# Perceiver block on one core: first attention's scores from four 64-row matmuls instead of three 128-row ones

## The chip, the cores and the metric

One core of a Trainium2 chip runs the whole block as one program. The time is the device time of the slowest core in microseconds, here of the only core. TensorE is PE in the rows (PEld its weight loads), VectorE DVE, ScalarE ACT, GpSimd POOL, SyncE SP.

## The reference, cut to what matters

The input x is 16 batches of 64 rows by 512, the context 16 batches of 512 rows by 512. A cross attention with 16 heads of 64, a self attention with 16 heads of 32, and a mixture of 8 experts (top 2) follow each other, each with a residual. The change touches the first attention's scores, and in the experts the place of one step:

```python
x = x + xattn(layernorm(x), ctx, ctx, ...)
    q = (query @ Wq + bq); k = (key @ Wk + bk); v = (value @ Wv + bv)
    scores = einsum('bqhd,bkhd->bhqk', q, k) / 8
    attn = softmax(scores); out = einsum('bhqk,bkhd->bqhd', attn, v)
x = x + attn(layernorm(x), ...)
x = x + ffn(layernorm(x), ...)
    h = gelu(x @ W1[e] + b1[e]); y = h @ W2[e] + b2[e]
```

## The kernel before, in words

Products are made at more than one pass's precision: each operand is split into a high part (fp32r) and a low part, and `split_pairs` (line 170) lists for each product high by high, high by low and low by high. `products` (line 405) issues them, so every logical 128x128x512 product is three matmuls.

**First attention** (lines 549 to 563). A pair of heads (128 columns of K) of one batch is one step; there are NS = 128 steps, 8 a batch. For step n TensorE runs, in this order: `project_k(n)` (12 matmuls of 512 columns into bank n % 2), `scores(n-1)` (3 matmuls), `project_v(n+4)` (12 matmuls, while n < 124), in every fourth step `weigh` (64 small matmuls of 64 columns, weights of 128 rows by 64 columns), and `turn(n-2)` (4 transposes of the probabilities into bank 6). For the scores the queries of a batch lie in `qbd`: for pair j a 128x128 matrix, the first head's queries in rows 0 to 63 and columns 0 to 63, the second head's in rows 64 to 127 and columns 64 to 127, zeros elsewhere, once as high and once as low part. Three matmuls of it with K (high, low) give the scores of both heads at once, 128x512, in bank 4 + n % 2. Two banks take turns.

ScalarE's order in step n (lines 1263 to 1297): at a batch's first step two splits of the next context (L1201), K's high part out of its bank (L1276), the exponential of scores n-1 (L1282, with the sum of each row), at a batch's third step `build_qbd` for the next batch (two copies of 64x512, L1252), in every fourth step the high part of `weigh`'s result (L1257), the copy of the transposed probabilities (L1292). VectorE's (lines 906 to 928): K's low part (L910), the row maximum of scores n-1 straight from the bank (L915), reciprocal and scaling (L917, L919), V out of its bank with its bias (L890), `build_qbd`'s low parts (L879), the low part of `weigh`'s result (L900). GpSimd splits the context and stores low parts. All order is by semaphores: `s_psum` (scores made), `s_max`, `s_exp`, `p_done` (probabilities ready), `k_lo`, `v_done`, `qbd_hi`, `qbd_lo`, `qbd_zero`.

**Experts.** A job is one expert: 16 tiles of the hidden width. In tile i TensorE runs `up` (12 matmuls as wide as the expert has rows, rounded up to one of eight widths), `down` of tile i - 3 (3 matmuls a 128 rows). Between them the next expert's rows are turned: `turned_at` (line 249) says after which tile each of the four 128-row chunks is transposed (`turn_rows`, line 715; ScalarE's copy `rows_high`, L1415; VectorE's `rows_low`, L1141). All four use bank 7, so chunk c waits for chunk c-1 to be out. The rows are gathered by GpSimd's queue (`fetch_rows`, L1588) into `xg`, which is also the tile that the expert before sends its results from (L1601), so the gather starts when those have been sent. ScalarE and VectorE also split the next expert's weights (L1201, L827), loaded tile by tile on SP's queue (L270).

Of the kernel before, what the change touches and what calls it, by code (L numbers as in the profile page):

```python
# [7 lines left out]
F32 = mybir.dt.float32  # L8
F32R = mybir.dt.float32r
# [3 lines left out]
ALU = mybir.AluOpType  # L13
ACT = mybir.ActivationFunctionType
AX = mybir.AxisListType.X
KB = 1024
P = 128


def perceiver_block(nc, a, out):  # L20

    B, TB, D = 16, 64, 512
# [4 lines left out]
    H1, HD1 = 16, 64  # L27
    HV = H1 * HD1
    NJ = HV // P
# [8 lines left out]
    with ExitStack() as stack:  # L38
        base = -(-nc.sbuf_base // 64) * 64

        def place(name, kb, shape, dt=F32):
            return nc.alloc_sbuf_tensor_at(name, shape, dt, offset=base + int(kb * KB))

        psum = stack.enter_context(nc.psum_tensor("psum", [P, 8, 512], F32))
        bank = [psum[:, i, :] for i in range(8)]
# [45 lines left out]
        o = c0 + 108  # L91
# [3 lines left out]
        xnT = [place(f"xnT{i}", o + 32 + 16 * i, [P, KD, T], F32R) for i in range(2)]  # L95
        Wq = [place(f"Wq{i}", o + 64 + 16 * i, [P, KD, HV], F32R) for i in range(2)]

        qbd = [[place(f"qbd{r}{i}", o + 32 + 8 * r + 4 * i, [P, NJ, P], F32R) for i in range(2)] for r in range(2)]
        kT = [[place(f"kT{r}{i}", o + 48 + 4 * r + 2 * i, [P, NKEY], F32R) for i in range(2)] for r in range(2)]
        V = [place(f"V{r}", o + 56 + 8 * r, [P, NKT, 512]) for r in range(3)]  # L100
        Pr = [place(f"Pr{r}", o + 80 + 2 * r, [P, NKEY]) for r in range(2)]
# [68 lines left out]
        def split_pairs(lhs, rhs):  # L170

            return [p for (lh, ll), (rh, rl) in zip(lhs, rhs) for p in ((lh, rh), (lh, rl), (ll, rh))]

        def pair(x, *idx):
            return (x[0][idx], x[1][idx])
# [71 lines left out]
        LAG = 3  # L247

        def turned_at(i):
            return {7: 0, 9: 1, 11: 2, 13: 3}.get(i)  # L250

        def d_on(i, k):
            return 0 <= i - k < NT
# [150 lines left out]
        def tensor_program(pe):  # L404
            def products(dst, pairs):
                for n, (l, r) in enumerate(pairs):
                    mm = pe.matmul(dst, l, r, start=n == 0, stop=n == len(pairs) - 1)  # L407
                return mm
# [89 lines left out]
            def scores(n):  # L498
                b, j = divmod(n, NJ)
                if j == 0:  # L500
                    pe.wait_ge(qbd_lo, 2 * b + 2)
                pe.wait_ge(k_lo, n + 1)
                if n >= 2:
                    pe.wait_ge(s_exp, n - 1)
                else:
                    pe.wait_ge(v_done, 3 + n)
                products(bank[4 + n % 2], split_pairs([pair(qbd[b % 2], slice(None), j)], [(kT[n % 2][0][:], kT[n % 2][1][:])])
                         ).then_inc(s_psum, 1)

            def turn(n):  # L510
                pe.wait_ge(p_done, n + 1)
# [19 lines left out]
            def c_product(t):  # L531
                rows = slice(t * P, (t + 1) * P)
                pe.wait_ge(low_in[t % 4], 16 * (t // 4 + 1))
                if t == 0:
                    loaded(*range(L_WO, L_WO + 4))
                if t < 2:
                    pe.wait_ge(v_done, NS)
                elif t < 4:
                    pe.wait_ge(k_lo, NS)
                elif t < 6:  # L540
                    pe.wait_ge(s_exp, NS)
                elif t == 6:
                    pe.wait_ge(pT_done, NS)
                else:
                    pe.wait_ge(o_lo, NS // HALF)
                products(c_bank(t), split_pairs([(Ohi[:, j, rows], oT[t % 4][:, j, :]) for j in range(NJ)],
                                                  [pair(Wo, slice(None), j) for j in range(NJ)])).then_inc(c_psum, 1)
# [273 lines left out]
        def vector_program(v):  # L821
# [47 lines left out]
                    split_lo(L_WK + j - 5, Wk[1][:, j - 5, :], Wk[0][:, j - 5, :])  # L869
            v.wait_ge(q_psum, 2 * NJ)  # L870
            for r in range(2):
                for i in range(2):
                    v.memset(qbd[r][i][:].bitcast(F32), 0.0).then_inc(qbd_zero, 1)

            def build_qbd(b):
                for h in range(2):
                    rows, cols = slice(64 * h, 64 * h + 64), slice(64 * h, 64 * h + 64)
                    v.wait_ge(qbd_hi, 2 * b + h + 1)
                    v.tensor_tensor(qbd[b % 2][1][rows, :, cols], QO[rows, :, b * TB:(b + 1) * TB], qbd[b % 2][0][rows, :, cols],  # L879
                                    ALU.subtract).then_inc(qbd_lo, 1)  # L880

            def evict_v(n):
                u, kt = divmod(n, HALF)
                cs = slice((u % 2) * 512, (u % 2) * 512 + 512)
                v.wait_ge(v_psum, n + 1)
                if n == 0:
                    v.wait_ge(bv_in, 16)
                if u >= 3 and kt == 0:
                    v.wait_ge(o_psum, HALF * (u - 2))
                v.tensor_tensor(V[u % 3][:, kt, :], bank[2 + (n if n < HALF else n % 2)], bvb[:, cs], ALU.add).then_inc(v_done, 1)  # L890
# [8 lines left out]
                    v.wait_ge(low_out[u % 4], 16 * (u // 4))  # L899
                v.tensor_tensor(Olo[u % 4][:], bank[7][:, 0:HALF * TB].rearrange("p (s q) -> p s q", s=HALF), hi, ALU.subtract).then_inc(o_lo, 1)  # L900

            v.wait_ge(qbd_zero, 4)
            build_qbd(0)
            for n in range(HALF):
                evict_v(n)
            for n in range(NS + 1):
                b, j = divmod(n, NJ)
                if n < NS:
                    v.wait_ge(k_hi, n + 1)
                    v.scalar_tensor_tensor(kT[n % 2][1][:], bank[n % 2], bkc[:, j:j + 1], kT[n % 2][0][:], ALU.add, ALU.subtract  # L910
                                           ).then_inc(k_lo, 1)
                if n >= 1:
                    m, r = n - 1, (n - 1) % 3
                    v.wait_ge(s_psum, m + 1)
                    v.tensor_reduce(smn[:, r:r + 1], bank[4 + m % 2], AX, ALU.max, negate=True).then_inc(s_max, 1)  # L915
                    v.wait_ge(s_exp, m + 1)
                    v.reciprocal(srec[:, r:r + 1], ssum[:, r:r + 1]).then_inc(s_recip, 1)  # L917
                    v.wait_ge(s_recip, m + 1)
                    v.tensor_scalar(Pr[m % 2][:], Pr[m % 2][:], srec[:, r:r + 1], None, ALU.mult).then_inc(p_done, 1)  # L919
                if n + HALF < NS:  # L920
                    evict_v(n + HALF)
                if j == 2 and b + 1 < B:
                    build_qbd(b + 1)
                if n >= 6 and n % HALF == 2:
                    o_low(n // HALF - 1)
                if n in (NS - 4, NS - 2):
                    for c in (n - NS + 4, n - NS + 5):
                        split_lo(L_WO + c, Wo[1][:, 2 * c:2 * c + 2, :], Wo[0][:, 2 * c:2 * c + 2, :])
# [267 lines left out]
        def scalar_program(s):  # L1196
# [50 lines left out]
            def build_qbd(b):  # L1247
                if b >= 2:
                    s.wait_ge(s_psum, NJ * (b - 1))
                for h in range(2):  # L1250
                    rows, cols = slice(64 * h, 64 * h + 64), slice(64 * h, 64 * h + 64)
                    s.activation(qbd[b % 2][0][rows, :, cols], QO[rows, :, b * TB:(b + 1) * TB], ACT.Copy).then_inc(qbd_hi, 1)  # L1252

            def o_high(u):
                b, half = divmod(u, 2)
# [2 lines left out]
                             ACT.Copy).then_inc(o_hi, 1)  # L1258

            s.wait_ge(q_done, 2 * NJ)  # L1260
            s.wait_ge(qbd_zero, 4)
            build_qbd(0)
            for n in range(NS + 3):
                b, j = divmod(n, NJ)
                if n < NS:
                    if j == 0 and b + 1 < B:
                        if n:
                            s.wait_ge(k_psum, n)
                            s.wait_ge(v_psum, n)
                        else:  # L1270
                            s.wait_ge(norm_out, 16)
                        ctx_high(b + 1)
                    s.wait_ge(k_psum, n + 1)
                    if n >= 2:
                        s.wait_ge(s_psum, n - 1)
                    s.activation(kT[n % 2][0][:], bank[n % 2], ACT.Identity, bias=bkc[:, j:j + 1]).then_inc(k_hi, 1)  # L1276
                if 0 <= n - 1 < NS:
                    m, r = n - 1, (n - 1) % 3
                    s.wait_ge(s_max, m + 1)
                    if m >= 2:  # L1280
                        s.wait_ge(pT_psum, m - 1)
                    s.activation(Pr[m % 2][:], bank[4 + m % 2], ACT.Exp, bias=smn[:, r:r + 1], accum_out=ssum[:, r:r + 1]).then_inc(s_exp, 1)  # L1282
                if n < NS and j == 2 and b + 1 < B:
                    build_qbd(b + 1)
                if n >= 6 and n % HALF == 2 and n < NS + 2:
                    o_high(n // HALF - 1)
                if 0 <= n - 2 < NS:
                    m = n - 2
                    s.wait_ge(pT_psum, m + 1)
                    if m >= HALF:  # L1290
                        s.wait_ge(o_psum, m - HALF + 1)
                    s.activation(PT[m % HALF][:], bank[6], ACT.Copy).then_inc(pT_done, 1)  # L1292
                if n in (NS - 4, NS - 2):
                    if n == NS - 4:
                        s.wait_ge(v_psum, NS)
                    for c in (n - NS + 4, n - NS + 5):
                        split_high(L_WO + c, Wo[0][:, 2 * c:2 * c + 2, :])
# [412 lines left out]
```

## Time and profile before

| | us |
|---|---|
| runs shown (3) | 1736.29, 1738.79, 1741.46; median 1738.79 |
| profiled execution, its own time | 1740.04 |
| its span in the trace | 1738.2 |
| PE / PEld / DVE / ACT / POOL busy | 1650.6 / 1391.5 / 881.5 / 696.1 / 307.2 |
| mean granted TensorE clock | 0.973 of full |

The profiled execution lies 1.25 us above the median of the runs, and its span 1.8 us below its own time. Busy time of PE counts a matmul from its start to its modelled end (389 ns for 512 columns), though the next may start 227 ns after it; what a matmul takes of the span is read from starts. Stages in the order of time: query projection to 49 us, first attention to 977, output product and second attention to 1210, experts to 1738.

### The profile page before, as it was taken

Reading aid. Unit: us, or ns where it says so; the run is one execution under the profiler, and the core shown is the slowest. Engines: PE = TensorE matmul, PEld = TensorE weight load, DVE = VectorE, ACT = ScalarE, POOL = GpSimd, SP = SyncE. Lnnn points to the kernel's source line nnn. Section 1 sums busy time; section 2 is a strip of 40 time slices with the busy share of each in tenths; the row PEclk is TensorE's granted clock in tenths of the full one; section 3 lists DMA queues with packets and bytes.
Section 4 is the critical chain, followed back from the end, with each engine's and each line's share of the span. In section 5 each row is a group of like instructions: output and inputs, shape, how many; then the busy total and the mean of one; then the engine's idle time right before and its main releaser. Section 6 shows DMA issues by size and latency. Waiting matters only on the chain. (4 is left out here: it accounts for less than half of the span.)

```text
span 1738.2 us, 26944 instructions
## 1 busy us (share of the span) xinstructions
PE 1650.6 (95%) x10858; PEld 1391.5 (80%) x10858; DVE 881.5 (51%) x1592; ACT 696.1 (40%) x1314; POOL 307.2 (18%) x258
## 2 busy tenths in 40 slices
PE   7999999999999999999999987995899999999987
PEld 6888888888888888888888766774888888888876
DVE  4344434443444434443443575785777457548842
ACT  5333333333333333333333433453655345436531
POOL 3201210011101110111010061465311011101101
PEclk9999999999999999999999998996899999999799
DMA  6601830111011101111002460113756336537621
GB/s 222 203 31 52 130 75 7 53 56 53 8 51 56 52 20 40 55 52 39 24 4 80 147 195 25 51 57 124 261 155 213 127 97 225 152 92 232 211 50 21
DMA packets 54101, 165.16 MB, mean 95 GB/s; under 512 B 10612, under 2 KB 10996, under 8 KB 53408
## 3 DMA queue, kind: packets, MB, share of 16 engines
q1 hardware_dynamic: 38032, 131.88, 22.3%
q0 software_dynamic: 15920, 31.19, 8.5%
q8 instruction: 106, 1.74, 0.4%
q14 instruction: 43, 0.35, 0.1%
HBM read 143.54 MB, written 55.64 MB: 115 GB/s over the span
## 5 line engine op out<-in xcount | busy, mean ns | idle before, releaser
L407 PE MATMUL psum<-ctx,Wk 128*128 128x512 f32 x1536 | 384.9, 399 | 0.0
L407 PE MATMUL psum<-Wv,ctx 128*128 128x512 f32 x1536 | 368.7, 389 | 0.0
L407 PEld LDWEIGHTS psum<-Wv,ctx 128*128 128x128 f32 x1536 | 288.3, 188 | 59.7
L407 PEld LDWEIGHTS psum<-ctx,Wk 128*128 128x128 f32 x1536 | 279.2, 188 | 55.5
L910 DVE SCALAR_TENSOR_TENSOR kT<-psum,bkc,kT 128x512 fp32r<-128x512 f32 x128 | 96.0, 750 | 387.7 <-ACT kT L1276 387.7
L407 PE MATMUL psum<-xgT,Wh 128*128 128x224 f32 (+5 forms) x1536 | 253.6, 319 | 13.1 <-issue 13.1
L407 PEld LDWEIGHTS psum<-xgT,Wh 128*128 128x128 f32 x1536 | 232.0, 200 | 30.9 <-issue 15.9
L748 PE MATMUL psum<-Wh,hs 128*128 128x512 f32 x981 | 246.4, 396 | 0.0
L748 PEld LDWEIGHTS psum<-Wh,hs 128*128 128x128 f32 x981 | 181.4, 191 | 34.1 <-DVE hs L1164 0.4
L1276 ACT ACTIVATE kT<-psum,bkc 128x512 fp32r<-128x512 f32 x128 | 88.3, 690 | 247.1 <-PE psum L407 247.0
L1441 ACT ACTIVATE gl<-psum,b1c 128x512 f32<-128x512 f32 x128 | 87.8, 686 | 211.5 <-PE psum L407 211.5
L1282 ACT ACTIVATE Pr<-psum,smn 128x512 f32<-128x512 f32 x128 | 88.2, 689 | 186.0 <-DVE smn L915 186.0
L827 DVE TENSOR_TENSOR Wh<-raw,Wh 128x1024 fp32r<-128x1024 f32 x128 | 155.6, 1219 | 7.1 <-ACT Wh L1201 6.9
L1504 POOL DMA_DIRECT2D low_parts<-Olo x32 | 24.5, 767 | 712.0 <-DVE Olo L900 712.0
L1201 ACT ACTIVATE Wh<-raw 128x1024 fp32r<-128x1024 f32 x128 | 134.4, 1054 | 26.8 <-DMA raw<-in_W 26.2
L1162 DVE CAST hs<-gl 128x512 fp32r<-128x512 f32 x128 | 55.3, 432 | 137.3 <-ACT gl L1441 136.6
L1292 ACT ACTIVATE PT<-psum 128x512 f32<-128x512 f32 x128 | 76.6, 598 | 97.0 <-PE psum L412 97.0
L407 PE MATMUL psum<-kT,qbd 128*128 128x512 f32 x384 | 107.9, 389 | 0.0
L1601 POOL DMA_INDIRECT out_x<-xg,meta x22 | 36.9, 1676 | 390.1 <-DVE xg L1154 387.4
L1477 POOL TENSOR_TENSOR ctx<-raw,ctx 128x1024 fp32r<-128x1024 f32 x32 | 76.1, 2399 | 113.1 <-ACT ctx L1201 113.1
L1164 DVE TENSOR_TENSOR hs<-gl,hs 128x512 fp32r<-128x512 f32 x128 | 88.7, 693 | 4.4
L890 DVE TENSOR_TENSOR V<-psum,bvb 128x512 f32<-128x512 f32 x128 | 87.4, 683 | 3.5 <-PE psum L407 3.5
(149 smaller groups left out, 1787.0 us busy)
## 6 DMA issues: line engine op xcount, KB each, us to landing
raw<-in_W SPq DMA_DIRECT2D x128, 512.0 KB, 3.8
expert_rows<-in_spare_rows SPq DMA_DIRECT2D x16, 1042.0 KB, 7.4
raw<-in_ctxT SPq DMA_DIRECT2D x32, 512.0 KB, 4.4
xg<-expert_rows POOLq DMA_DIRECT2D x32, 256.0 KB, 5.6
low_parts<-Olo POOLq DMA_DIRECT2D x32, 128.0 KB, 2.4
oT<-low_parts SPq DMA_DIRECT2D x8, 512.0 KB, 5.1
out_x<-x SPq DMA_DIRECT2D x12, 256.0 KB, 2.2
xs<-in_x SPq DMA_DIRECT2D x4, 512.0 KB, 6.8
```

The source lines that it names most:

```text
L407: mm = pe.matmul(dst, l, r, start=n == 0, stop=n == len(pairs) - 1)
L748: mm = pe.matmul(bank[3 + c], hr[x][:, c * P:(c + 1) * P], Wh[i][y][:, 512:1024], start=i == 0 and m == 0, stop=i == NI - 1 and m == 2)
L827: v.tensor_tensor(lo, src, hi, ALU.subtract).then_inc(split_done[r], 1)
L890: v.tensor_tensor(V[u % 3][:, kt, :], bank[2 + (n if n < HALF else n % 2)], bvb[:, cs], ALU.add).then_inc(v_done, 1)
L910: v.scalar_tensor_tensor(kT[n % 2][1][:], bank[n % 2], bkc[:, j:j + 1], kT[n % 2][0][:], ALU.add, ALU.subtract).then_inc(k_lo, 1)
L1164: v.tensor_tensor(lo, gl[n % HS][:], hi, ALU.subtract).then_inc(h_lo, 1)
L1201: s.activation(hi, src, ACT.Copy).then_inc(split_hi, 1)
L1276: s.activation(kT[n % 2][0][:], bank[n % 2], ACT.Identity, bias=bkc[:, j:j + 1]).then_inc(k_hi, 1)
L1282: s.activation(Pr[m % 2][:], bank[4 + m % 2], ACT.Exp, bias=smn[:, r:r + 1], accum_out=ssum[:, r:r + 1]).then_inc(s_exp, 1)
L1292: s.activation(PT[m % HALF][:], bank[6], ACT.Copy).then_inc(pT_done, 1)
L1441: s.activation(gl[n % HS][:], bank[n % 3], ACT.Gelu, bias=b1c[:, col:col + 1]).then_inc(gelu_done, 1)
L1477: g.tensor_tensor(lo, src, hi, ALU.subtract).then_inc(split_done[r], 1)
```

## The change

It rearranges the operands of the scores. `qbd` keeps only the high parts (block-diagonal, zeros elsewhere). A new `qx` holds in each 64-row half the same high part in the head's own columns and the low part in the other head's columns. For each head h the rows 64h to 64h+63 alone are multiplied: `qx` with K's high part, then `qbd` with K's low part, both into bank 4 + h. So a bank holds a head's scores in its own 64 partitions and the part low by high in the other 64. ScalarE copies that part across to the head's partitions of `Pr`, VectorE adds the two, and takes the maximum from `Pr`; the exponential reads `Pr` too. Banks 4 and 5 serve every step, no longer turn by turn. V's eviction stands ahead of reciprocal and scaling in VectorE's order. In the experts each chunk of rows is turned one tile later. `s_max` now counts three a step (two additions and the maximum), `s_exp` three (two copies and the exponential), `qbd_hi` four a batch.

```diff
-        qbd = [[place(f"qbd{r}{i}", ...) for i in range(2)] for r in range(2)]
+        qbd = [place(f"qbd{r}", o + 32 + 8 * r, [P, NJ, P], F32R) for r in range(2)]
+        qx = [place(f"qx{r}", o + 36 + 8 * r, [P, NJ, P], F32R) for r in range(2)]
...
         def turned_at(i):
-            return {7: 0, 9: 1, 11: 2, 13: 3}.get(i)
+            return {8: 0, 10: 1, 12: 2, 14: 3}.get(i)
...
             def scores(n):
                 b, j = divmod(n, NJ)
                 if j == 0:
+                    pe.wait_ge(qbd_hi, 4 * b + 4)
                     pe.wait_ge(qbd_lo, 2 * b + 2)
                 pe.wait_ge(k_lo, n + 1)
-                if n >= 2:
-                    pe.wait_ge(s_exp, n - 1)
+                if n:
+                    pe.wait_ge(s_max, 3 * n - 1)
                 else:
-                    pe.wait_ge(v_done, 3 + n)
-                products(bank[4 + n % 2], split_pairs([pair(qbd[b % 2], slice(None), j)], [(kT[n % 2][0][:], kT[n % 2][1][:])])
-                         ).then_inc(s_psum, 1)
+                    pe.wait_ge(v_done, HALF)
+                for m, (q, k) in enumerate(((qx[b % 2], kT[n % 2][0]), (qbd[b % 2], kT[n % 2][1]))):
+                    for h in range(2):
+                        rows = slice(HD1 * h, HD1 * (h + 1))
+                        mm = pe.matmul(bank[4 + h], q[rows, j, :], k[rows, :], start=m == 0, stop=m == 1)
+                mm.then_inc(s_psum, 1)
...
             for r in range(2):
-                for i in range(2):
-                    v.memset(qbd[r][i][:].bitcast(F32), 0.0).then_inc(qbd_zero, 1)
+                v.memset(qbd[r][:].bitcast(F32), 0.0).then_inc(qbd_zero, 1)
...
-                    v.tensor_tensor(qbd[b % 2][1][rows, :, cols], QO[...], qbd[b % 2][0][rows, :, cols],
+                    v.tensor_tensor(qx[b % 2][rows, :, other], QO[...], qbd[b % 2][rows, :, cols],
...
                     m, r = n - 1, (n - 1) % 3
-                    v.wait_ge(s_psum, m + 1)
-                    v.tensor_reduce(smn[:, r:r + 1], bank[4 + m % 2], AX, ALU.max, negate=True).then_inc(s_max, 1)
-                    v.wait_ge(s_exp, m + 1)
+                    for h in range(2):
+                        rows = slice(64 * h, 64 * h + 64)
+                        v.wait_ge(s_exp, 3 * m + h + 1)
+                        v.tensor_tensor(Pr[m % 2][rows, :], bank[4 + h][rows, :], Pr[m % 2][rows, :], ALU.add).then_inc(s_max, 1)
+                    v.wait_ge(s_max, 3 * m + 2)
+                    v.tensor_reduce(smn[:, r:r + 1], Pr[m % 2][:], AX, ALU.max, negate=True).then_inc(s_max, 1)
+                if n + HALF < NS:
+                    evict_v(n + HALF)
+                if n >= 1:
+                    v.wait_ge(s_exp, 3 * m + 3)
                     v.reciprocal(srec[:, r:r + 1], ssum[:, r:r + 1]).then_inc(s_recip, 1)
                     v.wait_ge(s_recip, m + 1)
                     v.tensor_scalar(Pr[m % 2][:], Pr[m % 2][:], srec[:, r:r + 1], None, ALU.mult).then_inc(p_done, 1)
-                if n + HALF < NS:
-                    evict_v(n + HALF)
...
-                for h in range(2):
-                    s.activation(qbd[b % 2][0][rows, :, cols], QO[...], ACT.Copy).then_inc(qbd_hi, 1)
+                for dst in (qbd[b % 2], qx[b % 2]):
+                    for h in range(2):
+                        s.activation(dst[rows, :, cols], QO[...], ACT.Copy).then_inc(qbd_hi, 1)
...
-                    s.wait_ge(s_max, m + 1)
+                    s.wait_ge(s_psum, m + 1)
                     if m >= 2:
                         s.wait_ge(pT_psum, m - 1)
-                    s.activation(Pr[m % 2][:], bank[4 + m % 2], ACT.Exp, bias=smn[:, r:r + 1], accum_out=ssum[:, r:r + 1]).then_inc(s_exp, 1)
+                    for h in range(2):
+                        rows, other = slice(64 * h, 64 * h + 64), slice(64 - 64 * h, 128 - 64 * h)
+                        s.activation(Pr[m % 2][rows, :], bank[4 + h][other, :], ACT.Copy).then_inc(s_exp, 1)
+                    s.wait_ge(s_max, 3 * m + 3)
+                    s.activation(Pr[m % 2][:], Pr[m % 2][:], ACT.Exp, bias=smn[:, r:r + 1], accum_out=ssum[:, r:r + 1]).then_inc(s_exp, 1)
```

The output product's waits for the score banks (`s_exp` there becomes `s_max`, three times the count) and the two waits for `qbd_zero` (2 for 4) follow from this.

## Rows read from the trace of the kernel before

**Rows 1.** Busy time of each engine by stage (windows), with clock and DMA.
```profile
0.00:49.00 49.00, 36.23 (x225) 33.22 (x226) 19.57 (x38) 26.53 (x36) 19.71 (x16) 1.00 0.64 224
49.00:977.00 928.00, 927.10 (x6013) 768.68 (x6011) 376.28 (x705) 331.78 (x614) 103.09 (x65) 1.00 0.18 53
1210.00:1738.00 528.00, 488.61 (x2672) 429.90 (x2672) 324.53 (x443) 242.10 (x316) 76.46 (x80) 0.95 0.52 155
```

**Rows 2.** Timeline of one step of the first attention; start us, us, engine, line, operation.
```profile
500.83 3.02 PE L407 MATMUL psum<-ctx,Wk 128*128 128x512 f32 x12
503.69 0.84 PE L407 MATMUL psum<-kT,qbd 128*128 128x512 f32 x3
503.89 0.69 ACT L1276 ACTIVATE kT<-psum,bkc 128x512 fp32r<-128x512 f32 x1 [2.17 <-PE psum L407]
504.37 2.88 PE L407 MATMUL psum<-Wv,ctx 128*128 128x512 f32 x12
504.61 0.75 DVE L910 SCALAR_TENSOR_TENSOR kT<-psum,bkc,kT 128x512 fp32r<-128x512 f32 x1 [3.13 <-ACT kT L1276]
505.28 0.68 DVE L915 TENSOR_REDUCE smn<-psum 128x1 f32<-128x512 f32 x1
505.99 0.69 ACT L1282 ACTIVATE Pr<-psum,smn 128x512 f32<-128x512 f32 x1 [1.42 <-DVE smn L915]
507.09 0.60 PE L412 MATMUL psum<-ident,Pr 128*128 128x128 f32 x4
507.44 3.00 PE L407 MATMUL psum<-ctx,Wk 128*128 128x512 f32 x12
507.72 0.60 ACT L1292 ACTIVATE PT<-psum 128x512 f32<-128x512 f32 x1 [0.95 <-PE psum L412]
```

**Rows 3.** Timeline where weights change from 128x128 to 128x64 (weigh).
```profile
405.72 0.39 PE L407 MATMUL psum<-Wv,ctx 128*128 128x512 f32 x1
...
406.04 0.13 PEld L527 LDWEIGHTS psum<-PT,V 128*64 128x64 f32 x1 [0.35 <-issue]
```

**Rows 4.** Line 527 (weigh) alone: durations ns min/median/max, idle time before.
```profile
L527 PE MATMUL psum<-PT,V x2048: 222/222/270, 120.2 to 997.7; 128*64 128x64 f32 x187
...
  issue: 10.9, 31
```

**Rows 5.** Timeline from 128x128 weights to 32x64 (second attention's scores), and inside them.
```profile
1162.44 0.39 PE L407 MATMUL psum<-Wa,o 128*128 128x512 f32 x1
...
1180.41 0.76 PE L609 MATMUL psum<-kT,qT 32*64 32x64 f32 x40
```

**Rows 6.** Line 609 (second attention's scores) alone.
```profile
L609 PE MATMUL psum<-kT,qT x512: 217/217/265, 1057.5 to 1181.0; 32*64 32x64 f32 x171
...
  issue: 2.5, 7
```

**Rows 7.** Timeline back from 128x64 weights to 128x128.
```profile
997.59 0.34 PE L527 MATMUL psum<-PT,V 128*64 128x64 f32 x6
997.87 0.50 PE L407 MATMUL psum<-Wo,Ohi 128*128 128x512 f32 x1
```

**Rows 8.** Groups of ScalarE and VectorE in the first attention: busy us, mean ns, idle before.
```profile
L1252 ACT ACTIVATE qbd<-QO 64x512 fp32r<-64x512 f32 x32 | 19.9, 623 | 4.2 <-DVE qbd L873 3.8
...
L879 DVE TENSOR_TENSOR qbd<-QO,qbd 64x512 fp32r<-64x512 f32 x32 | 21.8, 682 | 1.3 <-ACT qbd L1252 0.8
```

**Rows 9.** What TensorE waited for in the experts from 1300 us on.
```profile
PE psum L407 <- issue: 8.8, 4, 5.5
PE psum L412 <- DMA xg<-expert_rows: 5.4, 3, 2.9
PE psum L412 <- DVE xgT L1141: 3.2, 1, 3.2
```

**Rows 10.** Timeline of TensorE and ScalarE around the turned rows.
```profile
1445.06 0.66 PE L412 MATMUL psum<-ident,xg 128*128 128x128 f32 x4 [2.32 <-DMA xg<-expert_rows]
...
1628.74 1.06 ACT L1201 ACTIVATE Wh<-raw 128x1024 fp32r<-128x1024 f32 x1 [3.15 <-DMA raw<-in_W]
...
1631.80 1.08 PE L412 MATMUL psum<-ident,xg 128*128 128x128 f32 x4 [3.24 <-DVE xgT L1141]
```

**Rows 11.** Windows of the experts at full and at half clock.
```profile
1446.00:1449.50 3.50, 3.50 (x15) 3.11 (x14) 1.59 (x3) 2.04 (x3) 0.00 (x0) 0.51 0.90 273
...
1632.00:1651.00 19.00, 19.00 (x79) 17.63 (x79) 14.36 (x20) 9.66 (x13) 0.00 (x0) 0.50 0.53 169
```

More of the change, by code:

```diff
@@ L96, in perceiver_block @@
         Wq = [place(f"Wq{i}", o + 64 + 16 * i, [P, KD, HV], F32R) for i in range(2)]
-        qbd = [[place(f"qbd{r}{i}", o + 32 + 8 * r + 4 * i, [P, NJ, P], F32R) for i in range(2)] for r in range(2)]
+        qbd = [place(f"qbd{r}", o + 32 + 8 * r, [P, NJ, P], F32R) for r in range(2)]
+        qx = [place(f"qx{r}", o + 36 + 8 * r, [P, NJ, P], F32R) for r in range(2)]
         kT = [[place(f"kT{r}{i}", o + 48 + 4 * r + 2 * i, [P, NKEY], F32R) for i in range(2)] for r in range(2)]
@@ L540, in c_product @@
                 elif t < 6:
-                    pe.wait_ge(s_exp, NS)
+                    pe.wait_ge(s_max, 3 * NS)
                 elif t == 6:
@@ L871, in vector_program @@
             for r in range(2):
-                for i in range(2):
-                    v.memset(qbd[r][i][:].bitcast(F32), 0.0).then_inc(qbd_zero, 1)
+                v.memset(qbd[r][:].bitcast(F32), 0.0).then_inc(qbd_zero, 1)
             def build_qbd(b):
                 for h in range(2):
-                    rows, cols = slice(64 * h, 64 * h + 64), slice(64 * h, 64 * h + 64)
-                    v.wait_ge(qbd_hi, 2 * b + h + 1)
-                    v.tensor_tensor(qbd[b % 2][1][rows, :, cols], QO[rows, :, b * TB:(b + 1) * TB], qbd[b % 2][0][rows, :, cols],
+                    rows, cols, other = slice(64 * h, 64 * h + 64), slice(64 * h, 64 * h + 64), slice(64 - 64 * h, 128 - 64 * h)
+                    v.wait_ge(qbd_hi, 4 * b + h + 1)
+                    v.tensor_tensor(qx[b % 2][rows, :, other], QO[rows, :, b * TB:(b + 1) * TB], qbd[b % 2][rows, :, cols],
                                     ALU.subtract).then_inc(qbd_lo, 1)
@@ L900, in o_low @@
                 v.tensor_tensor(Olo[u % 4][:], bank[7][:, 0:HALF * TB].rearrange("p (s q) -> p s q", s=HALF), hi, ALU.subtract).then_inc(o_lo, 1)
-            v.wait_ge(qbd_zero, 4)
+            v.wait_ge(qbd_zero, 2)
             build_qbd(0)
@@ L1249, in build_qbd @@
                     s.wait_ge(s_psum, NJ * (b - 1))
-                for h in range(2):
-                    rows, cols = slice(64 * h, 64 * h + 64), slice(64 * h, 64 * h + 64)
-                    s.activation(qbd[b % 2][0][rows, :, cols], QO[rows, :, b * TB:(b + 1) * TB], ACT.Copy).then_inc(qbd_hi, 1)
+                for dst in (qbd[b % 2], qx[b % 2]):
+                    for h in range(2):
+                        rows, cols = slice(64 * h, 64 * h + 64), slice(64 * h, 64 * h + 64)
+                        s.activation(dst[rows, :, cols], QO[rows, :, b * TB:(b + 1) * TB], ACT.Copy).then_inc(qbd_hi, 1)
             def o_high(u):
@@ L1260, in scalar_program @@
             s.wait_ge(q_done, 2 * NJ)
-            s.wait_ge(qbd_zero, 4)
+            s.wait_ge(qbd_zero, 2)
             build_qbd(0)
```

## The prediction

> **What bounds the kernel.** I read the windows by stage first. In the first attention (49 to 977 us, over half the span) TensorE is busy 927.1 of 928 us at full clock, DVE and ACT 376 and 332 [rows 1]: the stage is as long as TensorE's list of work. Then one step of it [rows 2]: it lasts from 500.83 to 507.44, 6.61 us, and no PE row shows idle time. Starts tell what each part takes of it: the 3 score matmuls from 503.69 to 504.37, 0.68 us, 0.227 us each; V's 12 the same 0.227 us each. ACT and DVE wait for TensorE in every step. In the experts TensorE is busy 488.6 of 528 us [rows 1], and the list of its waits has, from 1300 us on, 5.4 us for the gathered rows in 3 waits and 3.2 us in one for DVE's low part of the turned rows [rows 9]. So the scores' change is priced by TensorE's spacing alone, as long as the other engines keep up; the later turning is priced by those waits.
>
> **The scores, TensorE.** Before: 3 x 0.227 = 0.68 us. After: four matmuls of 64 rows. If the two halves of the array work side by side, they cost two spacings, 0.45 us. Do they? The second attention's scores use 32-row weights in four row groups: 40 matmuls in 0.76 us, of which 0.22 is the last one's own duration [rows 5, 6], so 0.0135 us each, four in 0.054 us. That is what one 64-column weight load and matmul would take, so row groups work side by side in this kernel, also into two banks. I take two spacings: **-0.23 us a step**.
>
> But the weights' shape changes, from 128x128 to 64x128 and back, in every step. The trace has no 64x128 weights; the nearest rows are other changes of shape. Into 128x64 (weigh): the last V matmul starts at 405.72, the first weight load at 406.04, 0.32 us apart where the spacing is 0.227 [rows 3]; 31 such idle times are named as issue, 10.9 us, 0.35 us each from the last weight load's end [rows 4]. Into 32x64: from 1162.44, with 7 such, 2.5 us, 0.36 each [rows 5, 6]. Semaphores had long been raised. So TensorE empties before the new shape, **+0.09 us**, whatever the new shape is. And the first load after it isn't hidden: the first matmul of a group lasts 270 or 265 ns instead of 222 or 217 for 64 columns [rows 4, 6]. For 128 columns the row is the way back, where the first matmul of 512 columns lasts 0.50 us against 0.39 [rows 7, 3]: **+0.11 us**. A change of shape costs 0.20 us, a step has two, +0.40. With -0.23 and about 0.005 for the second half's start: +0.18 us a step, 128 steps: **+23 us**.
>
> The bounds of this term. Below: row halves alone need no emptying and the loads stay hidden: -0.227 x 128 = -29 us. Between: emptying, but loads hidden: 2 x 0.09 - 0.227 = -0.05 us, -6 us. Above: the two halves' first loads go one after the other, +0.11 more a step, +14, so +37 us. I take +23 since both known shapes, a column half and row quarters, show the same gap in and the same kind of load after it. The Trainium skill has both sides of it. "TensorEngine Tiling (Array Packing)", Key Properties, says that changing the tiling mode, not just the tile, drains TensorE, and it lists 64x128 as a mode of its own; by that, and these rows' gap agrees, the term is +23. "TensorE: Matmul & The Clock Gate", Part 3, gives a pack of tiles the duration of one matmul and some 4 ns a further tile, and speaks of no price for coming and going; by it alone the term would be -29.
>
> **The scores, ACT and DVE: nothing, while TensorE covers them.** ACT gets two copies of 64x512 a step; the nearest are build_qbd's 623 ns [rows 8], so +1.25 us in a step in which it idles 2.17 + 1.42 + 0.95 = 4.5 us [rows 2]. DVE gets two additions of about 0.68 us [rows 8]. In time from a step's start: K's high part 3.06 to 3.75; the scores are out at about 3.8 as well; copies to 5.0; DVE has K's low part done at 4.5, additions to about 5.9, maximum to 6.6, exponential to 7.3, copy of the turned ones to 7.9, still ahead of K's next high part at 6.8 + 3.06 = 9.85. V's eviction can start when V is made, 6.65, ends 7.35; reciprocal and scaling to 8.2, for a turn at 13. The new wait is that of scores n for the additions of step n-1, since banks 4 and 5 are used each time: raised at 5.9, needed at 9.6, 3.7 us to spare. Behind it on TensorE would queue V's matmuls and everything else. A batch's third step has two more copies (1.25 us) and weigh: the turned copy then ends about 2 us late, its user comes 5 us after. What covers all this is V's 12 matmuls; they are missing in steps 124 to 126, where a step is 3.9 us and ACT's list 4.9 with its waits: +1 us each, and VectorE's split of Wo just behind them waits in the same queue: **+2 us** (0 to +5). Two memsets less and DVE ahead at the start: DVE waits there for TensorE, 0.
>
> **Rows turned a tile later.** PE, ACT and DVE all move by the same tile, and no DMA is moved past another: the gather's issue hangs on the results sent and on the turned rows of the job before. In a narrow expert a tile is 2.95 us or more, so the waits for gathered rows (2.3 and 2.9 us, and 0.2) are gone: **-5.4 us** [rows 9, 10]. After the first the clock fell to half for 3.5 us [rows 11], so **-1.7** more. The 3.2 us wait is another: ACT stood in its queue 3.15 us for a weight load (till 1628.74) and took the turned chunk only then, PE's second chunk waited for it at 1631.80 [rows 10]. One tile later PE has an up and a down in between, and then waits itself for the late gelu, about 1 us: **-2.2**. After that wait stand 19 us at half clock [rows 11]: at full clock they would be some 10 us. Whether the clock falls without the longer wait no row tells; none of the three job starts with 0.8 to 1.3 us of idle (part of the 8.8 us of issue) was followed by a fall, one of the two 2.3 to 2.9 us waits was. I take half of a gain that is held down by the weight loads, 7 us: **-3.5** (0 to -9). Sum **-13 us** (-6 to -18). The last chunk's low part is due 5 us before the next job needs it and comes 2 to 3 later: 0.
>
> **Sum.** +23 + 2 - 13 = +12 us on the profiled execution's 1740.0, 1752; the median of runs is 1.25 lower, so 1751.
>
> **Rivals.**
> 1. *The halves need no emptying* (the other sign): adding over 64 rows rather than 128 may be set by the matmul itself. It decides at the change from Wk's last matmul to the first score matmul, and back: if each costs under 0.11 us, the stage shrinks. Then -29 + 2 - 13: 1700; with emptying and hidden loads -6 + 2 - 13: 1722. For it: no row shows 64x128. Against: both shapes that are shown pay it each time, in and out. Chances 0.14 and 0.06.
> 2. *First loads one after the other*: 1751 + 14 = 1765. For: 128 columns of two halves in one go, unseen. Against: the four row groups' loads of line 609 start together. 0.08.
> 3. *The change doesn't do what it says*: the halves run in turn, four spacings and not two, +0.45 us a step, +58: 1809. Against it stands line 609. 0.03.
> 4. *ACT and DVE become the bound*, scores waiting for additions: needs 3.7 us of lateness in a usual step. 0.02; with 1 us a step over, 128 us more.
> The forecast as stated has 0.67, with its own range 1740 to 1763 from the bounds of the tail and of the turning.
>
> **Numbers.** A measurement here can tell 0.3%, 5.2 us. Slower than 1744: most of the forecast's 0.67 and rivals 2 to 4: 0.71. Faster than 1733.6: rival 1 and a corner: 0.21. Range 1736 to 1770: the forecast and rival 2; it leaves out rivals 1, 3 and 4.
>
> **What would show it.** In the changed profile: a step's length 6.79 us against 6.61; from Wk's last matmul to the first score matmul 0.32 us, the first of the four about 0.50 us long, the next pair 0.23 later, then 0.32 to V's first, also 0.50 long. PE without idle rows between 49 and 960. ACT's copies near 0.6 us, right behind K's high part. In the experts no wait for xg but the first job's, and the half-clock stretch shorter or gone. Wrong if the gaps around the scores are 0.23 (rival 1), if the four start 0.23 apart (rival 3), or if PE has idle rows with DVE Pr as their releaser (rival 4).

## Result and the profile after

The changed kernel takes 1761.88 us (median of 4 runs, 1760.21 to 1763.94) against 1737.54 of the kernel before in the same sessions: ratio 1.0153, 95% interval 1.0127 to 1.018. It is slower by 24.3 us; forecast was 1751 in 1736 to 1770, with 0.71 for slower. So the way and the range came true, but the change is twice the 12 us that were forecast. The profiled execution's span is 1758.6 us against 1738.2.

The windows by stage again (us, then busy time of PE, PEld, DVE, ACT and POOL, clock, DMA):

```profile
49.00:977.00 928.00, 928.00 (x5962) 706.32 (x5961) 536.58 (x924) 475.36 (x867) 101.28 (x63) 1.00 0.18 52
...
1240.00:1758.00 518.00, 485.10 (x2672) 426.87 (x2672) 323.05 (x444) 241.41 (x315) 76.50 (x80) 0.95 0.53 158
```

In the same 928 us [rows 1] TensorE is as full as before, with 51 matmuls fewer begun though each step has one more; DVE and ACT have 160 and 144 us more and stay near half busy. So the time is to be looked for in how far apart TensorE's matmuls start (their spacing). One step of the changed kernel, as [rows 2] shows one of before:

```profile
505.99 3.01 PE L408 MATMUL psum<-ctx,Wk 128*128 128x512 f32 x12
...
508.92 0.19 PEld L512 LDWEIGHTS psum<-kT,qx 64*128 64x128 f32 x2 [0.35 <-issue]
508.92 0.50 PE L512 MATMUL psum<-kT,qx 64*128 64x512 f32 x2
...
509.03 0.69 ACT L1286 ACTIVATE kT<-psum,bkc 128x512 fp32r<-128x512 f32 x1 [1.24 <-PE psum L408]
509.26 0.40 PE L512 MATMUL psum<-kT,qbd 64*128 64x512 f32 x2
509.58 2.60 PEld L408 LDWEIGHTS psum<-Wv,ctx 128*128 128x128 f32 x12 [0.36 <-issue]
509.58 3.03 PE L408 MATMUL psum<-Wv,ctx 128*128 128x512 f32 x12
509.74 1.21 ACT L1294 ACTIVATE Pr<-psum 64x512 f32<-64x512 f32 x2
...
510.42 1.40 DVE L921 TENSOR_TENSOR Pr<-psum,Pr 64x512 f32<-64x512 f32 x2
511.85 0.69 DVE L923 TENSOR_REDUCE smn<-Pr 128x1 f32<-128x512 f32 x1
512.22 0.59 PEld L413 LDWEIGHTS psum<-ident,Pr 128*128 128x128 f32 x4
512.45 0.60 PE L413 MATMUL psum<-ident,Pr 128*128 128x128 f32 x4
512.57 0.72 ACT L1296 ACTIVATE Pr<-Pr,smn 128x512 f32<-128x512 f32 x1 [1.62 <-DVE smn L923]
...
512.80 1.41 PE L408 MATMUL psum<-ctx,Wk 128*128 128x512 f32 x5
```

The step is 512.80 - 505.99 = 6.81 us, before 6.61. The score matmuls start in two pairs, 0.34 apart, each pair side by side. No weight load starts until 0.35 us after the last one of K ended, and again before V's. The first pair lasts 0.50 us instead of 0.39, and V's 12 matmuls reach from 509.58 to 512.45, 2.87 us instead of 2.72. The line of the scores alone, over all 128 steps:

```profile
L512 PE MATMUL psum<-kT,qx x256: 463/493/494, 83.6 to 1014.0; 64*128 64x512 f32 x128
...
L512 PE MATMUL psum<-kT,qbd x256: 392/392/393, 84.0 to 1014.3; 64*128 64x512 f32 x128
its engine sat idle before it (us, times) until:
  issue: 47.0, 128
  DVE Pr L921: 1.9, 1
```

128 idle times of the weight loads, 47.0 us, 0.37 each: every step pays it, and in only one step did TensorE wait for VectorE's additions.

Where the 20.4 us between the two spans lie, by starts in the traces (us), with the experiments of the next section beside them. The first column (first to last matmul of V) is called the steady part below, the second the last steps, and the fourth (from the first turned expert rows) the expert stage:

| | first to last V matmul | last V to first of output product | from there to first turned expert rows | experts to the end |
|---|---|---|---|---|
| before | 892.5 | 20.0 | 239.6 | 520.9 |
| after | 918.8 | 25.1 | 239.0 | 511.3 |
| e1 rows turned later, old scores | 892.5 | 20.0 | 239.4 | 511.3 |
| e2 new scores, rows as before | 918.8 | 24.6 | 239.9 | 524.3 |
| e3 two whole matmuls | 864.7 | 24.6 | 239.1 | 516.5 |
| e4 other order of halves | 919.6 | 24.6 | 238.8 | 512.4 |
| e5 weigh beside the scores | 913.4 | 24.6 | 238.4 | 510.8 |
| e6 turned after 8, 11, 13, 15 | 892.5 | 20.0 | 240.0 | 507.5 |
| e7 turned after 9, 11, 13, 15 | 892.5 | 20.0 | 237.9 | 512.0 |
| e8 four whole matmuls | 920.4 | 24.7 | 237.3 | 511.3 |

After against before: +26.3, +5.0, -0.6, -9.6, and -0.6 ahead of the first V matmul: +20.4 (each is rounded by itself).

### The profile page after: what moved, and what is told of

It is laid out like the page before. It is cut to its first block and busy times, and to the rows that moved or that the text cites. A ratio compares the mean times of both kernels' runs of the same rounds, so it can differ in the third digit from the quotient of the medians.

```text
span 1758.6 us, 27758 instructions
## 1 busy us (share of the span) xinstructions
PE 1675.2 (95%) x10986; PEld 1346.4 (77%) x10986; DVE 1062.3 (60%) x1846; ACT 859.5 (49%) x1602; POOL 306.9 (17%) x258
## 5 line engine op out<-in xcount | busy, mean ns | idle before, releaser
L408 PE MATMUL psum<-Wv,ctx 128*128 128x512 f32 x1536 | 386.1, 400 | 0.0
L408 PEld LDWEIGHTS psum<-Wv,ctx 128*128 128x128 f32 x1536 | 278.9, 188 | 99.1 <-issue 44.7
L1296 ACT ACTIVATE Pr<-Pr,smn 128x512 f32<-128x512 f32 x128 | 92.6, 724 | 208.4 <-DVE smn L923 208.4
L921 DVE TENSOR_TENSOR Pr<-psum,Pr 64x512 f32<-64x512 f32 x256 | 175.2, 684 | 6.9 <-ACT Pr L1294 2.9
L1294 ACT ACTIVATE Pr<-psum 64x512 f32<-64x512 f32 x256 | 151.6, 592 | 8.9 <-PE psum L512 2.5
## 6 DMA issues: line engine op xcount, KB each, us to landing
raw<-in_W SPq DMA_DIRECT2D x128, 512.0 KB, 4.2
raw<-in_ctxT SPq DMA_DIRECT2D x32, 512.0 KB, 4.4
oT<-low_parts SPq DMA_DIRECT2D x8, 512.0 KB, 5.0
xs<-in_x SPq DMA_DIRECT2D x4, 512.0 KB, 6.6
```

The lines of the kernel that those rows point to most:

```text
L921: v.tensor_tensor(Pr[m % 2][rows, :], bank[4 + h][rows, :], Pr[m % 2][rows, :], ALU.add).then_inc(s_max, 1)
L1294: s.activation(Pr[m % 2][rows, :], bank[4 + h][other, :], ACT.Copy).then_inc(s_exp, 1)
L1296: s.activation(Pr[m % 2][:], Pr[m % 2][:], ACT.Exp, bias=smn[:, r:r + 1], accum_out=ssum[:, r:r + 1]).then_inc(s_exp, 1)
```

## The experiments

**e1: the later turning alone.**

```diff
 # kernel before
-            return {7: 0, 9: 1, 11: 2, 13: 3}.get(i)
+            return {8: 0, 10: 1, 12: 2, 14: 3}.get(i)
```

> Kernel before, with the rows turned a tile later and nothing else. My theory (the later turning is worth what the two traces show between the experts' first turn and their last up, 501.9 us before and 492.4 after): 9 to 10 us shorter than before, ratio 0.994 to 0.995, the two waits for gathered rows gone, the wait for the turned rows' low part of about 3 us still there and about 20 us at half clock behind it. Rival (the gain comes only with the longer first attention, which shifts the loads): within 3 us of before.

Measured: ratio 0.9961 (0.9938 to 0.9985), 1731.0 against 1737.9. The expert stage is 9.6 us shorter in the trace. TensorE's waits there, to be read beside [rows 9]:

```profile
PE psum L407 <- issue: 8.4, 4, 5.4
PE psum L412 <- DVE xgT L1141: 3.6, 1, 3.6
PE psum L412 <- DMA xg<-expert_rows: 0.9, 2, 0.7
PE psum L748 <- DVE hs L1164: 0.3, 1, 0.3
```

The waits for gathered rows fell from 5.4 to 0.9 us, the one for the turned rows is still there (3.6 us, before 3.2), as expected. The stretch at half clock behind it was 10.2 us in this run, not 20; in the changed kernel it was 20.5 behind a wait of 2.9 us. The windows at half clock, e1's first, then the changed kernel's:

```profile
1627.30:1637.50 10.20, 10.20 (x46) 9.51 (x43) 9.41 (x13) 5.47 (x8) 0.00 (x0) 0.50 0.56 202
...
1653.60:1674.10 20.50, 18.95 (x78) 17.60 (x78) 15.84 (x23) 11.29 (x16) 0.00 (x0) 0.50 0.54 177
```

So its length doesn't follow from the wait's. One trace of this stage is a rough measure: from the first expert's first up matmul to the second's, the six traces with this turning (the changed kernel, e1, e3, e4, e5, e8) have 63.0 to 69.5 us. By the medians of the runs the later turning is worth 6.9 us, by the trace 9.6.

**e2: the scores alone** (the changed kernel with `{7: 0, 9: 1, 11: 2, 13: 3}`).

> Changed kernel with the rows turned where they were. My theory: the scores cost 0.21 us a step (26 us for 124 steps) and 5 us in the last steps, so 31 us over before, ratio 1.018, the experts as long as before (501.9 us). Rival: the parts don't add, the experts lose or gain several us with the scores.

Measured: ratio 1.0184 (1.0134 to 1.0233), 1771.7. The steady part is 918.8 us as in the changed kernel, the last steps are 24.6 (25.1). The two parts together, +33.8 and -6.9, make +27 against +24.3 for the whole: they add up within the intervals. The experts were expected to be as long as before and took 524.3 us against 520.9, with two waits for gathered rows of 5.2 and 3.3 us (before 2.3 and 2.9): these waits differ by some us between runs.

**e3: two matmuls over all rows in place of four over halves.**

```diff
-                for m, (q, k) in enumerate(((qx[b % 2], kT[n % 2][0]), (qbd[b % 2], kT[n % 2][1]))):
-                    for h in range(2):
-                        rows = slice(HD1 * h, HD1 * (h + 1))
-                        mm = pe.matmul(bank[4 + h], q[rows, j, :], k[rows, :], start=m == 0, stop=m == 1)
+                for h, (q, k) in enumerate(((qx[b % 2], kT[n % 2][0]), (qbd[b % 2], kT[n % 2][1]))):
+                    mm = pe.matmul(bank[4 + h], q[:, j, :], k[:], start=True, stop=True)
```

> Changed kernel, but each step's four 64-row matmuls are two of all 128 rows, one a bank, so half of the sums is not what the reference has (the other head is added in and the low part of K goes to one bank only); copies, additions, waits and order stay. No change of weight shape is left. My theory (the cost is the change of shape, 0.09 us of emptying, 0.11 us of an open load and 0.03 us of wider spacing after it, twice or once): a step is one spacing shorter than before, 6.38 us against 6.61, V's matmuls start 0.227 us apart with the first 0.39 long, the stage 124 x 0.227 = 28 us shorter than before in its steady part and 54 us shorter than the changed kernel's; in all 1738 - 28 + 5 - 9 = 1706. Rival (ScalarE's and VectorE's added work costs the time, by waits or by contention for PSUM): the step stays at or above 6.61 us, or V's spacing stays wider than 0.227.

Measured: 1707.9 us, ratio 0.9826 (0.9783 to 0.9869). The steady part is 864.7 us: 27.8 below before, which is one spacing for each of the 123 score groups in it (0.227 x 123 = 27.9), and 54.1 below the changed kernel. This run has the changed kernel's two spacings of scores and all of its copies and additions, only without the change of shape. Its step:

```profile
502.16 0.39 PE L510 MATMUL psum<-kT,qx 128*128 128x512 f32 x1
...
502.38 0.39 PE L510 MATMUL psum<-kT,qbd 128*128 128x512 f32 x1
...
502.61 2.88 PE L408 MATMUL psum<-Wv,ctx 128*128 128x512 f32 x12
503.07 1.21 ACT L1292 ACTIVATE Pr<-psum 64x512 f32<-64x512 f32 x2
...
505.42 1.95 PEld L530 LDWEIGHTS psum<-PT,V 128*64 128x64 f32 x64 [0.35 <-issue]
```

V's 12 matmuls are back at 2.88 us in all, ScalarE's and VectorE's work is what it is in the changed kernel, and idle time as issue stands only before weigh, as it did before. So the price is the change of shape: 54.1 / 123 = 0.44 us a step, for two changes. ScalarE and VectorE cost nothing in the steady part. In the last steps they do: 24.6 us here as well, without any change of shape around the scores. The run leaves out that the two heads are kept apart.

**e4: the order of the halves.**

```diff
-                for m, (q, k) in enumerate(...):
-                    for h in range(2):
+                for h in range(2):
+                    for m, (q, k) in enumerate(...):
```

> Changed kernel with the four matmuls in the order head 0 twice, then head 1 twice. My theory (row halves run side by side only where neighbours in the order are of different halves, TensorE takes them in order): spacings of 0.34, 0.00 and 0.23 instead of 0.00, 0.34 and 0.00, so one spacing more a step, 0.23 us, 29 us in all, about 1790. Rival (the halves are independent queues and the order doesn't matter): as the changed kernel, 1762.

My expectation fell: 1760.8 us in one run, and a steady part of 919.6 us against 918.8. The timeline:

```profile
508.16 0.39 PE L408 MATMUL psum<-ctx,Wk 128*128 128x512 f32 x1
508.48 0.50 PE L512 MATMUL psum<-kT,qx 64*128 64x512 f32 x2
508.81 0.40 PE L512 MATMUL psum<-kT,qbd 64*128 64x512 f32 x2
```

The program gives head 0's `qx` and `qbd` products first, then head 1's. The two `qx` products, first and third, start within 0.01 us of each other, and the two `qbd` products, second and fourth, 0.33 us later. A matmul of one row half starts before an earlier one of the other half. The Trainium skill ("TensorE: Matmul & The Clock Gate", Part 3) calls matmuls strictly first in, first out, in start and end; for two row halves these starts differ from that, and the measurement decides. On the order of the ends these rows say nothing, since the profile's ends of matmuls are modelled.

**e5: weigh right behind the scores.**

```diff
-                if n + HALF < NS:
-                    project_v(n + HALF)
                 if n >= 6 and n % HALF == 2:
                     weigh(n // HALF - 1)
+                if n + HALF < NS:
+                    project_v(n + HALF)
```

> Changed kernel with weigh (128x64 weights) moved from behind V's matmuls to right behind the scores (64x128 weights), every fourth step. My theory (each change of weight shape empties TensorE and opens one load, also between two kinds of parts of the array): scores to weigh costs 0.09 + 0.05, weigh to V 0.09 + 0.11 + 0.03, and V to the turns nothing; the 0.14 into weigh and the 0.15 out of it that fell after V are replaced by 0.14 in and the 0.23 that V had anyway, so 0.15 us less in each of 31 such steps, -5 us, the last scores matmul to weigh's first load 0.32 us apart. Rival (only changes from or to the whole array empty it): 0.23 us apart, -8 us.

Measured: 1752.5 us, 1.0085 (1.0056 to 1.0114) of before. The steady part went from 918.8 to 913.4 us, -5.4 (expected -5); the spans of the two profiled executions differ by 7.4 us, since each of the other stages is 0.4 to 0.6 us shorter too, and the medians by 9.4. TensorE's weight loads in such a step:

```profile
497.19 0.18 PEld L512 LDWEIGHTS psum<-kT,qx 64*128 64x128 f32 x2 [0.35 <-issue]
497.30 0.19 PEld L512 LDWEIGHTS psum<-kT,qbd 64*128 64x128 f32 x2
497.85 1.95 PEld L532 LDWEIGHTS psum<-PT,V 128*64 128x64 f32 x64 [0.36 <-issue]
499.86 0.76 PEld L408 LDWEIGHTS psum<-Wv,ctx 128*128 128x128 f32 x4
```

From 64x128 weights to 128x64 the load waits as long (0.36) as from the whole array to 64x128 (0.35), so the rival falls: the gap comes with a change between two kinds of parts too, not only with one from or to the whole array.

**e6 and e7: where the rows are turned**, both on the kernel before: chunks after tiles 8, 11, 13, 15 (e6) and 9, 11, 13, 15 (e7).

```diff
-            return {7: 0, 9: 1, 11: 2, 13: 3}.get(i)
+            return {8: 0, 11: 1, 13: 2, 15: 3}.get(i)    # e7: {9: 0, 11: 1, 13: 2, 15: 3}
```

> Kernel before with the four chunks of rows turned after tiles 8, 11, 13 and 15 instead of 7, 9, 11 and 13. My theory (the wait of 3.2 to 3.6 us in the 128-wide expert is TensorE's second chunk waiting for ScalarE, which stands at a weight load, and the 20 us at half clock follow from that idle time): no wait over 1 us at the second chunk, no stretch at half clock behind it, so 3 us and some 7 us better than with 8, 10, 12, 14, 1722. Rival (the weight loads hold that expert anyway): the idle time turns up at the scores of up or down instead, about 1731.

> Kernel before with the chunks turned after tiles 9, 11, 13 and 15. My theory (the first turn waits for gathered rows only as long as these take to come, two tiles more are enough in each expert; the second chunk follows two tiles on as before): no wait for gathered rows, the second chunk's wait in the 128-wide expert shorter than 3 us since the weight load that ScalarE stood at has come, 1725 to 1731. Rival (the last chunk after tile 15 is late for the next expert or for ScalarE's bias step): idle time at the start of the experts, 1735 or more.

e6: ratio 0.9933 (0.9912 to 0.9955), 1724.2 us; e7: 0.995 (0.9929 to 0.9971), 1728.7. Both gain over the kernel before, and with it (they keep the old scores) lie 33 to 38 us under the changed kernel. Against e1 their intervals overlap. The mechanism that I expected of e6 came only in part:

```profile
1625.80 0.63 PE L412 MATMUL psum<-ident,xg 128*128 128x128 f32 x4 [0.86 <-DVE xgT L1141]
...
1632.99 0.86 PE L412 MATMUL psum<-ident,xg 128*128 128x128 f32 x4 [2.49 <-DVE xgT L1141]
```

The 3.6 us wait became 0.9, and 2.5 a chunk later; the half-clock stretch behind was 10.2 us, as long as in e1. e7 had no wait for gathered rows but the first job's, as expected, yet its wait at the second chunk was 3.8 us, not shorter. So no place of the turning that was tried frees the narrow expert; e6's rival, the weight loads, is nearer. ScalarE in the changed kernel, in the same expert:

```profile
1646.50 1.06 ACT L1210 ACTIVATE Wh<-raw 128x1024 fp32r<-128x1024 f32 x1 [2.62 <-DMA raw<-in_W]
...
1649.71 1.06 ACT L1210 ACTIVATE Wh<-raw 128x1024 fp32r<-128x1024 f32 x1 [1.57 <-DMA raw<-in_W]
...
1652.09 1.06 ACT L1210 ACTIVATE Wh<-raw 128x1024 fp32r<-128x1024 f32 x1 [0.75 <-DMA raw<-in_W]
1653.06 0.58 ACT L1429 ACTIVATE xgT<-psum 128x512 fp32r<-128x512 f32 x1
```

It waits for three weight loads one after the other and takes the first chunk 5.4 us after it was turned (at 1647.61). That the loads are slow because the gather of rows runs with them was not tested.

**e8: four matmuls over all rows** (`q[:, j, :]` and `k[:]`), a check of the sum.

> Changed kernel with the four matmuls over all 128 rows, so that the other head's products are added in (the output isn't the reference's); everything else stays. No change of shape, four spacings. My theory: a step is 6.61 + 0.227 = 6.84 us against 6.82 of the changed kernel, 1708 + 2 x 0.227 x 128 = 1766. Rival (ScalarE and VectorE are near their limit and a longer step hides some of their waits): under 1760.

1759.6 us in one run, just under the rival's bound of 1760. But the steady part says what it was to say: 920.4 us, 1.6 more than the changed kernel's 918.8, where 0.013 x 124 = 1.6 was expected, and 27.9 more than before, one spacing for each of 123 score groups; so the longer step hid no waits there. Of the 6 us short of 1766, 5 are e3's longer expert stage (516.5 against 511.3), from which I had counted. So the halves with their changes of shape cost what four products over the whole array cost.

## Why the prediction was right, and where it missed

The price of the change of shape, which gives the sign, was right in its parts. The size wasn't: three terms were off, all of them the same way, and together they are nearly as large as the 12 us that were forecast. The measured time still lies in the range, and just inside the forecast's own (1740 to 1763), whose upper end stands for dear last steps and a small gain from the turning. The last steps were that dear, but the turning gained more than that end allows for; the scores' 3.3 us and the 3.9 us by which the medians lie further apart than the two profiled executions took its place. So that the range held is in part luck. Rival 2 has no share in it: both loads of a pair start within 0.01 us (the row at 508.92), not one after the other.

- **Side by side, two spacings.** Right: pairs start together, the second 0.34 later, which is 0.227 and the open load. The step to it was weaker than it reads: that 0.054 us for four is what one load and matmul would take has no row behind it.
- **A change of shape empties TensorE, 0.09 us, whatever the shape.** Right: K's last matmul to the first score matmul 508.16 to 508.48 in e4, 0.32, and in the changed kernel the scores' second pair to V's first 509.26 to 509.58. Rival 1 was wrong; e3 shows what it would have brought (27.8 us less than before), and e5 that the gap belongs to the change itself. The Trainium skill's sentence that changing the tiling mode drains TensorE ("TensorEngine Tiling (Array Packing)", Key Properties) agrees, now also for 64x128, with 0.35 us from load to load.
- **The open load, 0.11 us.** Right: 493 ns against 392, and 0.50 for V's first.
- **Sum of the scores, 23 us.** It measured 26.3. The missing term is 0.03 us a step: behind the open load six of V's next spacings are 228 to 236 ns rather than 227, so that 12 take 2.87 us where 2.72 and 0.11 make 2.83. K's matmuls behind the turns had shown the like in the kernel before, 500.83 to 503.69 for 12, 2.86 us [rows 2], which I had read as a load alone.
- **The last steps, 2 us.** They measured 5.0. TensorE's waits there:

```profile
PE psum L512 <- DVE Pr L921: 1.9, 1, 1.9
PE psum L532 <- ACT PT L1306: 1.2, 1, 1.2
PE psum L413 <- DVE Pr L930: 0.5, 1, 0.5
```

  3.6 us against 1.4 before: the 2 us that I had. Behind them the clock stood at half:

```profile
998.20:1005.00 6.80, 5.72 (x71) 5.40 (x72) 4.45 (x9) 4.83 (x11) 0.05 (x1) 0.50 0.08 28
```

  It would be natural to put the rest down to the clock, but e3 speaks against it. Its last steps ran at full clock throughout and take 24.6 us all the same; TensorE waited 6.5 us there instead, last of all for VectorE's split of Wo. e3's window, its waits and that split:

```profile
928.80:953.40 24.60, 18.20 (x142) 14.30 (x142) 17.61 (x29) 16.29 (x29) 0.75 (x1) 1.00 0.20 66
...
PE psum L408 <- DVE Wo L830: 2.2, 1, 2.2
PE psum L510 <- DVE Pr L919: 1.9, 1, 1.9
PE psum L530 <- ACT PT L1304: 1.3, 1, 1.3
PE psum L413 <- DVE Pr L928: 1.1, 1, 1.1
...
950.81 2.36 DVE L830 TENSOR_TENSOR Wo<-raw,Wo 128x1024 fp32r<-128x1024 f32 x2 [0.56 <-ACT Wo L1208]
```

  e2, e4, e5 and e8 have 3.4 us at half clock and 24.6 or 24.7 us too. So without V's matmuls as cover the queues of ScalarE and VectorE set the length, 4.6 us over before, and the slow clock took the place of TensorE's waits; to the clock belongs at most the 0.5 us by which the changed kernel lies above the others. The term that was too small is "+1 us each, and VectorE's split of Wo just behind them waits in the same queue", set at 2 us: these queues cost 4.6, near the end of its bounds (0 to 5).
- **ACT and DVE cost nothing otherwise.** Right: copies 592 ns (I had 623), additions 684 (682), and e3.
- **Rows turned later, -13 us.** It measured -9.6. The two waits for gathered rows went, as forecast, with the half clock after the first of them. What failed is the step on the third wait, "One tile later PE has an up and a down in between, and then waits itself for the late gelu, about 1 us": it stayed at 2.9 us, with 20.5 us at half clock, since ScalarE stood at three weight loads before it took the first chunk. The 3.5 us from the clock and the 2.2 us of the wait didn't come. That leaves 7.1 us of the forecast, and from first up matmul to first up matmul the two experts in which the long waits for gathered rows stood are 3.6 and 3.3 us shorter. The rest of the 9.6 lies in pieces of at most 0.7 us ahead of the first expert and in the others, which is luck as far as the forecast goes: the same turning in e2 and before took 524.3 and 520.9 us.

The three misses, 3.3 + 3.0 + 3.4 = 9.7, less 1.2 us in parts that the change doesn't touch, lead from the forecast's +12 to the +20.4 of the spans. The medians of the runs lie 24.3 apart, 3.9 more than the two profiled executions.

## What to carry to other kernels

Part of the array runs beside another part, but coming to it and leaving it costs: here 0.20 to 0.22 us a change for 128-column weights. Splitting three 512-column products into two pairs saves one spacing (0.23 us) and pays two changes (0.44). By these numbers (an estimate, no run shows it) two saved spacings between two changes would about cover them, and only more than that would gain. What is added on idle engines stays free only where the cover stands; look at the last rounds of the loop, where the cover ends, and follow the queues of the other engines there up to the first product behind the loop. Before you price a stretch at half clock, ask what would have ended the wait at full clock: here the last steps took 24.6 us without one and 25.1 with 6.8 us of it.

## What was not expected of the hardware

- Matmuls of different row halves pass each other: in e4 the third in order starts with the first.
- 174 us more of VectorE's work and 157 us more of ScalarE's on PSUM and SBUF in the 864.7 us of e3's steady part left TensorE's spacing at 0.227 us.
- Behind an open load six of V's spacings are 1 to 9 ns longer than in the steady stream, 0.03 us in all.
- The stretches at half clock behind the wait at the narrow expert's second chunk were 10.2 us (waits of 3.6 in e1, 2.5 in e6, 3.8 in e7) or 20.5 us (2.9 in the changed kernel, 3.6 in e2): in this case neither follows from the other.
- In the last steps of the first attention 6.8, 3.4 or no us at half clock go with 25.1, 24.6 and 24.6 us: with the clock full, TensorE waited instead (e3).
